# Expert choice of three batches moved into the diffusion attention's last turn and drain, fills of the second gated network split, last norms on VectorE

## The reference, cut to what matters

```python
x = x + _layernorm(_L0_attn_ref(_layernorm(x), ...))
x = x + _layernorm(_L0_ffn_ref(_layernorm(x), ...))
x = x + _layernorm(_L1_attn_ref(_layernorm(x), ...))
x = x + _layernorm(_L1_ffn_ref(_layernorm(x), ...))
```

```python
gates = jax.nn.softmax(xf @ gate_w, axis=-1)
topw, topi = jax.lax.top_k(gates, K)          # K = 2 of E = 8 experts
topw = topw / jnp.sum(topw, axis=-1, keepdims=True)
combine = jnp.sum(topw[:, :, None] * jax.nn.one_hot(topi, E), axis=1)
h = jnp.einsum('td,edh->teh', xf, w1) + b1
h = _ln(h, ln1_g, ln1_b)
h = jax.nn.gelu(h, approximate=False)
y = jnp.einsum('teh,ehd->ted', h, w2) + b2
out = jnp.einsum('ted,te->td', y, combine)
out = _ln(out + xf, ln_g, ln_b)
```

## Time and profile before

| what | us |
|---|---|
| median of three runs | 4137.27 (4133.03 to 4146.78) |
| the profiled execution, its own time | 4133.88 |
| its span in the trace | 4132.2 |
| TensorE busy | 3681.5 (89%) |
| VectorE busy | 2371.7 (57%) |
| ScalarE busy | 1791.8 (43%) |
| GpSimd busy | 1668.0 (40%) |

### The profile page before, as it was taken

How to read it: one execution, slowest core, us unless ns; L and a number is a source line. 1 busy time by engine, 2 the same in 40 slices (tenths; PEclk the granted TensorE clock), 3 DMA queues, 4 the chain that set the end, 5 groups by cost and what they waited for, 6 DMA issues and landing times. The chain is left out here.

```text
span 4132.2 us, 60613 instructions
## 1 busy us (share of the span) xinstructions
PE 3681.5 (89%) x17520; PEld 2213.3 (54%) x17520; DVE 2371.7 (57%) x6484; ACT 1791.8 (43%) x4090; POOL 1668.0 (40%) x1891
## 2 busy tenths in 40 slices
PE   6999999999869999899899989868999999758995
PEld 3556555665535555555455555533555555445664
DVE  6676777677556564233566633425666666354556
ACT  2445454454425555211455542114555555303444
POOL 2343334343356665100676642431222221165664
PEclk8999999999889999999999999988999999958997
DMA  6655665566211111345011121122222222038993
GB/s 104 73 74 68 93 83 78 66 94 80 54 54 36 41 51 38 143 179 205 16 51 51 36 74 56 54 68 74 67 59 58 68 58 53 19 135 288 318 304 133
DMA packets 223891, 377.22 MB, mean 91 GB/s; under 512 B 39180, under 2 KB 155344, under 8 KB 217264
## 3 DMA queue, kind: packets, MB, share of 16 engines
q1 hardware_dynamic: 207776, 350.99, 36.0%
q0 software_dynamic: 6480, 17.77, 1.1%
q10 hardware_dynamic: 9408, 5.78, 0.5%
HBM read 169.64 MB, written 84.74 MB: 62 GB/s over the span
## 5 line engine op out<-in xcount | busy, mean ns | idle before, releaser
L758 DVE CUSTOM_DVE_ANT_0 a_ps<-a_ps,a_mask 128x128 f32<-128x128 f32 (+3 forms) x1024 | 479.6, 513 | 196.7 <-PE a_ps L513 179.0
L368 POOL TENSOR_SCALAR_AFFINE_SELECT a_probs_c<-a_probs_c 128x256 f32<-128x256 f32 (+1 forms) x384 | 187.3, 504 | 668.7 <-ACT a_probs_c L663 668.3
L2505 ACT ACTIVATE c_probsT<-c_ps 128x512 f32<-128x512 f32 x512 | 298.6, 601 | 327.6 <-PE c_ps L2327 318.4
L2644 DVE TENSOR_REDUCE c_neg_max<-c_ps 128x1 f32<-128x512 f32 x512 | 337.0, 683 | 151.1 <-PE c_ps L2315 149.7
L663 ACT ACTIVATE a_probs_c<-a_ps 128x512 f32<-128x512 f32 x640 | 344.9, 603 | 99.9 <-PE a_ps L531 70.7
L513 PE MATMUL a_ps<-a_packed_qk 65*128 65x128 f32 (+3 forms) x1024 | 339.4, 375 | 46.0 <-DVE a_maxima L758 26.9
L1101 POOL TENSOR_TENSOR w_probs<-w_probs,w_inv 128x1024 f32<-128x1024 f32 x128 | 242.3, 1893 | 334.6 <-DVE w_inv L1465 334.6
L549 PE MATMUL a_ps<-a_probs_c,a_v 128*64 128x512 f32 (+3 forms) x2048 | 318.6, 455 | 0.9 <-POOL a_probs_c L368 0.8
L531 PE MATMUL a_ps<-a_packed_qk 67*128 67x512 f32 (+3 forms) x1024 | 288.6, 345 | 2.2 <-DMA a_packed_qk<-a_max_half 2.1
L1356 ACT ACTIVATE w_probs<-w_ps_s,w_neg_max 128x256 f32<-128x256 f32 x512 | 235.9, 478 | 66.8 <-DVE w_neg_max L1460 66.1
L2315 PE MATMUL c_ps<-c_packed_qk 68*128 68x512 f32 x512 | 254.7, 503 | 11.2 <-DVE c_neg_max L2644 6.6
(11 more groups left out here) (355 smaller groups left out, 8052.1 us busy)
## 6 DMA issues: line engine op xcount, KB each, us to landing
a_packed_qk<-a_halves SPq DMA_DIRECT2D x512, 128.0 KB, 4.6
d_w<-in_L_ffn_second SPq DMA_DIRECT2D x71, 516.0 KB, 4.9
d_w<-in_L_ffn_first SPq DMA_DIRECT2D x71, 512.0 KB, 5.5
rows_dram<-f_zeros SPq DMA_DIRECT2D x8, 4128.0 KB, 16.1
c_packed_qk<-c_halves SPq DMA_DIRECT2D x256, 128.0 KB, 2.3
w_v<-w_v_next SPq DMA_DIRECT2D x16, 1024.0 KB, 4.7
d_rows<-rows_dram SPq DMA_DIRECT2D x71, 129.0 KB, 4.8
f_y_res<-y_dram SPq DMA_DIRECT2D x16, 512.0 KB, 3.9
```

Of the source, the lines that this page charges most:

```text
L758: last = nc.vector.tensor_tensor_reduce(tile, tile, mask[:, (NT - 1 - i) * P:], 1.0, -3e38, ALU.add, ALU.max, accum_out=maxima_of[:, hd // ...
L2505: nc.scalar.activation(probsT[:, q % 2, r, :], ps_again[u % 2][:, :], ACT.Exp).then_inc(exp_done.sem, 1)
L2644: nc.vector.tensor_reduce(neg_max[:, g % 2, 0, s % GS:s % GS + 1], bank("s", s)[:, :], AX.X, ALU.max, negate=True).then_inc(max_ready.sem, 1)
```

## The change

1. In a, f1 and c the last batch's norm, and in a and f1 the add after it, go to VectorE (`add_last`, `norm_last`); so do c's last add and the last `h` (`make_last`).
2. In both gated networks the next stage's loads are issued in turn 5, its statistics made in turn 6, and its fills are made in six parts, one in each of turns 0 to 5. Part p fills the heads from 16p/6 to 16(p+1)/6, that is 2, 3, 3, 2, 3 and 3 of them, one memset each; the last part also makes the other constants.
3. In c the expert choice of the first three batches (`EARLY = 3`) is made. Entries with distance `X` run in the last turn, those with `Y` in the drain: T statistics, N norm, H transposes, G gate products, S choice, P exponential, R ranks, L places; U and V are the statistics and norm of batch 3. SP loads the three inputs into buffers that c lends; GpSimd scatters their rows. `free` entries only count in the ring of banks.
4. d sorts the remaining five batches. Among the experts SP loads the three early inputs again, at blocks 8, 24 and 40, and VectorE norms them again, four tiles each, for the results.

```diff
+            def add_last(b):
+                dve.wait_ge(res_loaded.sem, res_loaded.at(b, 16))
+                dve.wait_ge(y_normed.sem, y_normed.at(b, 1))
+                nc.vector.tensor_tensor(x_res[:, :, :], x_res[:, :, :], y[:, :, :], ALU.add).then_inc(y_ready.sem, 1)
+            def norm_last(b):
+                roots_sum.wait(dve, b, 0)
+                for t in range(NT):
+                    last = normalise(nc, y[:, t, :], x_res[:, t, :], mv_y, rstd_y, t)
+                last.then_inc(normed_ready.sem, 1)
...
+                if b == B - 3:
+                    following.ahead_sync(sp)
...
-                if b + 3 == B:
-                    if LAST:
+                if b < B - 2:
+                    if LAST and b >= 1:
                         pool.wait_ge(y_ready.sem, y_ready.at(b - 1, 1))
                     pool.wait_ge(roots_in.ready.sem, roots_in.ready.at(b + 1, 1))
-                    following.ahead_fill(pool)
+                    following.ahead_fill(pool, b)
             if LAST:
                 pool.wait_ge(y_ready.sem, y_ready.at(B - 2, 1))
             following.ahead_gpsimd(pool)
             if LAST:
-                norm_output(B - 1)
...
-                    if c == 2 and b + 1 == B:
+                    if c == 2 and b + 2 == B:
...
+            def norm_last(b):
+                roots.wait(dve, b, 0)
+                out = following.handed
+                for t in range(NT):
+                    last = normalise(nc, out[:, t, :], yn[:, t, :], mv_y, rstd_y, t)
+                last.then_inc(normed.sem, 1)
+                dve.wait_ge(normed.sem, normed.at(b, 1))
+                dve.wait_ge(x_res_in.sem, x_res_in.at(b, 16))
+                nc.vector.tensor_tensor(out[:, :, :], out[:, :, :], x_res[:, :, :], ALU.add).then_inc(y_ready.sem, 1)
...
+    EXTRA = {0: [("m", 3, -1), ("H", (0, 0), Y), ("H", (0, 1), Y), ("free", 1, Y), ("free", 2, Y)], 2: [("q", 2, 0)],
+             4: [("free", 3, Y), ("G", 0, Y), ("free", 4, Y), ("free", 5, Y)],
...
+    AFTER_MAX = {5: [("q", 2, 0), ("S", 0, Y)], 10: [("q", 3, 0)], 12: [("L", 0, Y)], 14: [("n", 1, 0), ("S", 1, Y)],
...
+    FILLS = 6
+    def ahead_fill(pool, part):
+        heads = range(part * H // FILLS, (part + 1) * H // FILLS)
+        for hd in heads:
+            nc.gpsimd.memset(packed_qk[2 * ROWS:3 * ROWS, :, hd, :].bitcast(fp32), 1.0).then_inc(filled.sem, 1)
+        pool.wait_ge(filled.sem, (part + 1) * H // FILLS)
+        if part < FILLS - 1:
+            return
+        nc.gpsimd.memset(ones[:, :], 1.0).then_inc(made_pool.sem, 1)
...
-            body(B - 1, (-1, 0), False)
+            for j in (2, 3):
+                pack(B - 1, j, True)
+                pack_norms(B - 1, j)
+            sp.wait_ge(hn_ready.sem, hn_ready.at(B - 1, 1))
+            following.early_load(sp, 0)
+            sp.wait_ge(hT_psum.sem, hT_psum.at(B - 1, KD))
+            following.early_load(sp, 1)
             following.ahead_sync(sp)
+            following.early_load(sp, 2)
+            following.ahead_load(sp)
+            store(B - 2)
+            load_residual(B - 1)
+            following.early_landed(sp)
...
+                following.early_scatter(pool, 0, 0, 2 * NT)
+                following.early_root(pool, 2)
+                following.early_scatter(pool, 1, 0, 5)
                 root_between(b - 1)
-                following.ahead_gpsimd(pool)
-                norm_output(b - 1)
-            batches(pool, lambda: None, body, drain)
+                following.ahead_root(pool)
+                following.early_scatter(pool, 1, 5, 2 * NT)
+                following.early_scatter(pool, 2, 0, 2 * NT)
+                roots.step(pool, b - 1, 1, rstd[:, :], mv[:, :, 1], EPS, neg_half[:, :])
+                standing_wait(pool, roots.ready.sem, roots.ready.at(b - 1, 2), passed_pool.sem)
...
+    EARLY = 3
...
+    def early_load(sp, c):
+        if c >= 2:
+            sp.wait_ge(early_ready.sem, early_ready.at(c - 2, 1))
+        sp.dma_start(lent_x[c % 2][:, :, :], x_v[c]).then_inc(early_loaded[c % 2].sem, 16)
...
+    def early_turn(pe, c, k, out):
+        if k == 0:
+            pe.wait_ge(early_ready.sem, early_ready.at(c, 1))
+        for t in range(NT):
+            last = nc.tensor.transpose(out[:, t * P:(t + 1) * P], lent_h[c][:, t, 1 + k * P:1 + (k + 1) * P], ident[:, :])
+        last.then_inc(early_turned.sem, 1)
...
+    def early_scatter(pool, c, first, last):
+        if first == 0:
+            pool.wait_ge(early_placed.sem, early_placed.at(c, 1))
+        for n in range(first, last):
+            nc.gpsimd.indirect_dma_start(sorted_dram[:, :], bass.IndirectOffsetOnAxis(ap=place[:, c, n:n + 1], axis=0),
+                                         lent_h[c][:, n % NT, :], None).then_inc(early_sorted.sem, 16)
...
+            def load_again(b):
+                if b:
+                    sp.wait_ge(x_again.sem, x_again.at(b, 0))
+                sp.dma_start(x[b][:, :, :], x_v[b]).then_inc(x_again.sem, 16)
...
+            for s in range(LATE + 2):
+                if 0 < s < LATE:
                     roots_in.step(pool, s, 0, rstd_in[:, :], mv_in[:, :, 1], EPS, neg_half[:, :])
                 if s >= 2:
-                    scatter(s - 2)
+                    scatter(EARLY + s - 2)
...
+            def norm_again(b, t):
+                if t == 0:
+                    dve.wait_ge(x_again.sem, x_again.at(b, 16))
+                last = normalise(nc, h[b][:, t, 1:D + 1], x[b][:, t, :], early_mv[:, b, :, :], early_rstd[:, b, :], t)
+                if t == NT - 1:
+                    last.then_inc(h_again.sem, 1)
```

408 lines of the change are left out of this document (315 added, 93 removed), and 9 rows, old and new, of tables (AFTER_EXP, EXTRA).

## The result

The changed kernel took 4097.0 us in the median of four runs (4087.9 to 4102.8), the kernel before 4142.0 in the same four rounds (4133.0 to 4154.9). The ratio is 0.9885 with a 95% interval of 0.9857 to 0.9913: **45 us less, 36 to 59 by the interval**. Forecast were 63.5 us less and a range that began at 44 less. The direction is right, the size is not, and the time lies 4 us above the range (4057 to 4093). The kernel before was itself 4.7 us slower in these rounds than the 4137.3 that the range was counted from; by the saving alone, 45 us lies at the range's very edge.

The account below looks back on a forecast made before the run. TensorE was taken to bound the stages, chains of single operations the four seams (ends of a, f1 and c; d's sort). Terms summed to -63.5 us: 4070.4 on the profiled execution, 4074 on the median; range 4057 to 4093.

Parts of the forecast that it names:

- Last norms: Ends of a, f1 and c: norm and add moved from GpSimd to VectorE, 4.6 us less each, -13.7 together.
- Fills: f1, turns 1 to 5: splitting removes a 16.0 us loss, 8.7 comes back as norms alternate with fills; net -7.3 us.
- c's inputs: f1, turn 7: earlier loads and statistics of c's first input remove TensorE's wait; -18.9 us (17 to 19.5).
- c's last turn: Last turn of c: VectorE gains about 6.7 us of early-choice work, mostly hidden; +1 us (0 to 2).
- Drain: c's drain: early-choice work on TensorE +6.4 us (2 to 9), and waits behind the exponentials +1.5 (0.5 to 4).
- Rival 1: GpSimd's queue in c's drain: late batch 1 places delay root and second norm, about 12 us, time 4086; chance 0.15.
- Rival 4: c's normal turns: changed rotation of PSUM banks makes steps wait, slower at 4210 us; chance 0.02.
- The sort: Stage d: five batches sorted instead of eight saves 24 scatters and three roots; -35 us (-37 to -28).
- rival 2: Sort in d: the choice chain or the plan, not GpSimd, sets the end; saving about 20, time 4089; chance 0.1.
- Experts: Expert blocks: three inputs of 0.52 MB read again, 0 to 5.0 us, taken as +2.5; VectorE's norms hidden.
- Signs of being wrong: Drain over 15 us longer; last scatter to first block beyond a 22.1 us wait; GpSimd waiting on places, root behind.
- Chances: Whole kernel: faster 0.97, same 0.01, slower 0.02; forecast within 9 us 0.62.

Follow-up runs that it names:

- e1: Kernel after with stages c and d of before, so only the changes to a, f and c's earlier inputs; ratio 0.9908, 38 us less than before.
- e8: Kernel before, unchanged, run again for a second trace; a single execution of 4127.7 us.
- e9: Kernel before plus 8 unread matmuls of 8 columns after each of steps 4 and 12 of c's drain; 4150.8 us, drain 71.9 us.
- e3: Kernel after plus three unread 128x512 matmuls ahead of the gate products of early batches 0 and 1; 4097.5 us, ratio 0.9882.
- e4: Kernel after with the three inputs read again at the sort's start instead of at expert blocks 8, 24 and 40; 4091.5 us, ratio 0.9857.
- e7: Kernel after, unchanged, run again with a trace of its own; 4090.0 us, ratio 0.989.
- e10: Kernel before plus 2 unread matmuls of 512 columns after each of steps 4 and 12 of c's drain; 4143.0 us, drain 64.9 us.

## Why the prediction was wrong, by its steps

**Last norms** (three times -4.6): right, with 4.9, 4.7 and 5.1 us.

**Fills** (-7.3): right in mechanism. VectorE and GpSimd alternate, one operation for one fill. A fill cost 0.73 us instead of 0.86 and the turns 7.0 us instead of 8.7. That the cost was avoidable, by a wait for the norm ahead of the fill, the forecast didn't see.

**c's inputs** (-18.9): right to 0.1 us.

**c's last turn** (+1, 0 to 2): the work was right, the clock was left out. The turn's maxima end 2.0 to 4.1 us later in the eight traces with this turn (163.7 to 165.7 us over its last seven groups of maxima, against 161.6 in before and 161.7 in e1 and e8). Over these groups the granted clock has a mean of 0.99 in three of the eight, which is 1.7 us lost in 164, and they end 2.1 to 2.3 us later; it is 0.98 in the other five, 3.4 us lost, and they end 3.6 to 4.1 later. So 0.2 to 0.7 us are left for VectorE's added 6.7 us: they are hidden. Of the five traces without this turn four have a clock of 1.00; e9, whose turn is unchanged, has 0.99 and is 1.7 us longer. What takes the clock down in this turn isn't shown.

**Drain** (+7.9): the failed step. The forecast put batch 0's and 1's products at full clock, 1.8 us for a batch's gates, and wrote that the exponentials keep TensorE at full clock. It had the 9 us of "at half clock" as the bound for the added products alone. It missed that these products take the clock down for everything that stands beside them: in after `L2435` takes 1.94 us where it took 1.07, and the products of keys and queries and the transposes pay likewise. The measured +14.7 to +17.6 (mean 16.2) divides into two parts, by an estimate. The work can be read where the clock was mostly held: 76.6 - 5.6 - 62.4 = 8.6 us in e3, close to the 7.9 of the forecast. The rest, 7.6 us of the mean, is the clock's, about as large as the 7.0 between the narrow and the wide run. The part behind the exponentials, forecast at +1.5, was +1.0 to +1.3; what was missed lies in the exponentials, where the forecast had +6.4 and 13.6 to 16.7 were measured.

**Rival 1**, GpSimd's queue, named the place and a time nearer to the measured one (4086), but not the cause: the root never waited for a scatter. **Rival 4** didn't come: c up to its last turn took 1.0 us less. Its price of 0.3 us for a bank reused too early stands in no row and no run.

**The sort** (-35): -32.4 in the pair of traces, -35.6 in the means, so right; rival 2 didn't come. The plan was named as next to be late, with 8.6 us to spare that it would keep. In the traces with after's sort the plan's last operation starts between 3.2 us before and 1.9 us behind the start of the last scatter, and in the second trace of before 4.6 behind, so the 8.6 was a reading of one execution taken for a property.

**Experts** (+2.5, at most 5.0): the second step that failed, since the bound was wrong. It took a reload as 0.52 MB at the rate of the stretch, 1.65 us. The reload is issued ahead of a block's rows in SP's queue, with DMA 0.94 busy, and TensorE waits for these rows 2.1, 2.4 and 3.7 us, 8 to 9 us in all (9.5 by the means). e4 shows that it is the place.

**The end** (0): 3.4 us more behind the last store in every trace with after's stage d. The forecast had no term for it.

**Signs of being wrong.** The first one named came: the drain grew by over 15 us. The second, a wait of more than 22.1 us ahead of the first block, came in this trace (26.2) and not in e7 (21.4). The third came in words, a wait for places with the root behind it, and cost nothing.

**Chances.** 0.97 for faster was borne out. The range was too narrow because the drain's term ended at 9 + 4 and the experts' at 5, where 17 and 9 were measured.

## What to carry over

When small products are put between large ones, cost not only their own time but the clock of their neighbours, and try a form that moves many columns; it is tested quickly by products of both forms that nothing reads. A transfer that is needed late belongs where its queue is idle: at a DMA share of 0.94 each cost the wait of what stood behind it, 2.1 to 3.7 us where its bytes are 1.65. Where GpSimd's fills and VectorE's operations were released by the same event, a wait for the second ahead of the first was free (30.51 us a turn). And spare time read from one trace should be seen in a second one before a step rests on it.

## What was not expected of the hardware

- TensorE's granted clock fell from 1.00 to 0.50 while its rows were 9.5 to 9.7 of 10 us busy, behind 16 records of 8 columns (e9); 4 records of 512 columns in the same 1.9 us left it at 1.00 (e10).
- VectorE had waits of 0.2 to 2.5 us between dependent small operations near the end of the sort in twelve of the thirteen traces, 7 to 12 us together, in kernels with and without the change. The first trace of before had none.
- The end of the program behind its last store took 6.7 us in the five traces with before's stage d and 10.1 in the eight with after's.
- The time from the start to f1's first closing add, with the same instructions, differed by up to 18 us between executions; that is as much as the spread of whole runs (15 us in after's four).
